# Residual of the second feed-forward on GpSimd, a new order of VectorE's work, and the first turns through DRAM begun earlier

## What is computed

```python
# layer 0: one head
h = film(rmsnorm(x, norm1_w), cond, film1_w, film1_b)
x = x + softmax(Q(h) @ K(h).T / 16) @ V(h) @ proj_w + proj_b
h = film(rmsnorm(x, norm2_w), cond, film2_w, film2_b)
x = x + gelu(h @ mlp_w1 + mlp_b1) @ mlp_w2 + mlp_b2        # hidden 1024, exact gelu
# layer 1: 16 heads of 16 channels
x = x + gate_msa * (attention(modulate(ln(x), shift_msa, scale_msa)) @ w_proj + b_proj)
x = x + gate_mlp * (gelu(modulate(ln(x), shift_mlp, scale_mlp) @ w_mlp1 + b_mlp1) @ w_mlp2 + b_mlp2)
```

## Time and profile before

| what | value |
|---|---|
| median of 3 runs | 1588.21 us (1586.55 to 1589.85) |
| the profiled execution: its time, its span | 1593.56 us, 1591.7 us |
| busy: TensorE, VectorE, ScalarE, GpSimd | 98%, 82%, 53%, 30% |
| chain that ended last, by engine | TensorE 90%, VectorE 6%, ScalarE 2%, issue 1% |
| the same by line, largest | L208 63%, L1728 8%, L1710 7%, L1672 5% |
| mean granted TensorE clock | 0.992 of full speed |

### The profile page before, as it was taken

The page is one execution under the profiler, slowest core; times in us unless marked ns, Lnnn a source line. Parts: engine busy times, 40 slices in busy tenths (PEclk is TensorE's granted clock), DMA queues, the critical chain, the costliest instruction groups (busy, mean ns, idle before and its releaser), DMA issues.

```text
span 1591.7 us, 42636 instructions
## 1 busy us (share of the span) xinstructions
PE 1556.0 (98%) x14322; PEld 1393.5 (88%) x14322; DVE 1299.0 (82%) x2951; ACT 844.9 (53%) x1696; POOL 480.9 (30%) x639
## 2 busy tenths in 40 slices
PE   7999998999999998999999999999998999999999
PEld 7999998999999997777777777777766999999999
DVE  5798888687777777888888888888884888888886
ACT  3666664333333344677767677767765333333333
POOL 2333322131121223234334344333424222222221
PEclk9999999999999999999999999999998999999999
DMA  6600002111111112333333233333331233222222
GB/s 182 211 20 20 21 19 57 68 43 49 44 53 48 44 53 66 106 101 107 105 106 112 96 106 106 102 111 101 102 109 40 81 100 94 92 92 92 92 92 68
DMA packets 145922, 131.67 MB, mean 83 GB/s; under 512 B 23392, under 2 KB 128800, under 8 KB 145840
## 3 DMA queue, kind: packets, MB, share of 16 engines
q1 hardware_dynamic: 145680, 130.56, 25.9%
q0 software_dynamic: 160, 0.04, 0.1%
HBM read 54.09 MB, written 24.02 MB: 49 GB/s over the span
## 4 chain that ended last, share of the span: by engine, by line
PE 90%; DVE 6%; ACT 2%; issue 1%; DVEq 0%; DMA 0%; POOL 0%; ACTq 0%; SPq 0%
PE bank L208 63%; PE bank L1728 8%; PE bank L1710 7%; PE bank L1672 5%; PE bank L1738 2%; PE bank L390 2%; PE bank L1746 1%; PE bank L760 1%; PE bank L463 1%; DVE D_g_hi L1066 1%; PE bank L190 1%; DVE D_g_lo L1068 1%; ACT D_g L1058 0%; DVEq L340 0%; DMA A_w_film<-in_L_cond_film_w 0%
## 5 line engine op out<-in xcount | busy, mean ns | idle before, releaser
L1819 ACT ACTIVATE C_probs<-bank 128x1024 f32<-128x1024 f32 x256 | 262.4, 1025 | 156.3 <-PE bank L1710 156.0
L1684 DVE TENSOR_REDUCE C_negmax<-bank 128x4 f32<-128x1024 f32 x248 | 303.2, 1223 | 47.5 <-PE bank L1672 44.0
L1058 ACT ACTIVATE D_g<-bank,D_bias 128x256 f32<-128x256 f32 x256 | 107.3, 471 | 228.9 <-PE bank L208 210.9
L1058 ACT ACTIVATE B_g<-bank,B_bias 128x256 f32<-128x256 f32 x256 | 107.4, 471 | 222.9 <-PE bank L208 222.9
L357 POOL TENSOR_TENSOR m_small<-m_small,consts 128x2 f32<-128x2 f32 x64 | 48.1, 751 | 463.9 <-DVE m_small L348 236.2
L208 PE MATMUL bank<-D_wt_w_hi,D_g_lo 128*128 128x256 f32 x512 | 145.4, 284 | 4.4 <-DVE D_g_lo L1068 3.8
L208 PE MATMUL bank<-B_wt_w_hi,B_g_lo 128*128 128x256 f32 x512 | 143.7, 281 | 3.9 <-DVE B_g_lo L1068 3.7
L1710 PEld LDWEIGHTS bank<-C_qs,C_kx 64*128 64x128 f32 x1024 | 77.5, 185 | 78.1 <-ACT C_probs L1819 45.6
L208 PE MATMUL bank<-m_h_hi,D_wt_w_lo 128*128 128x256 f32 x512 | 143.3, 280 | 0.8 <-DVE m_h_lo L409 0.8
L208 PE MATMUL bank<-m_h_hi,B_wt_w_lo 128*128 128x256 f32 x512 | 142.7, 279 | 1.2 <-DVE m_h_lo L305 1.2
L208 PE MATMUL bank<-D_wt_w_lo,D_g_hi 128*128 128x256 f32 x512 | 142.8, 279 | 0.0
(11 more groups left out here) (263 smaller groups left out, 4918.5 us busy)
## 6 DMA issues: line engine op xcount, KB each, us to landing
C_qs<-C_q_hi SPq DMA_DIRECT2D x128, 128.0 KB
C_kx<-C_k_hi SPq DMA_DIRECT2D x128, 128.0 KB, 2.5
C_qs<-C_q_lo SPq DMA_DIRECT2D x64, 128.0 KB
C_kx<-C_k_lo SPq DMA_DIRECT2D x64, 128.0 KB, 2.2
C_gbc<-mod_rows SPq DMA_DIRECT2D x32, 256.0 KB, 3.3
D_gbc<-mod_rows SPq DMA_DIRECT2D x32, 256.0 KB, 3.4
out<-xres SPq DMA_DIRECT2D x31, 256.0 KB, 3.5
turned<-N_blocks SPq DMA_DIRECT2D x30, 256.0 KB, 2.0
```

The source lines that it names most:

```text
L1058: ins = eng.activation(o, p, func, bias=per_seq(bias1, 2 * u + d, b))
L1684: e_max.by(eng.tensor_reduce(m4[:, :, :, j], spair[:, :].rearrange("p (e q k) -> p e q k", e=2, q=TH), AX, ALU.max, negate=True))
L1819: e_exp.by(eng.activation(probs[t % NP][:, :], stpair[:, :], ACT.Exp, scale=scl))
```

## The change

- `residual` is new: in D, VectorE makes only `tmp`; xres = tmp + xb is one GpSimd instruction of 128x512, before `add_bias` in GpSimd's list.
- VectorE's order, in both feed-forwards: stats n, split 0, residual (D: `tmp`), split 1, evac_lo f, first half of normalize n, split 2, second half, turn n, split 3. In the first iteration stats of n come after split 1.
- ScalarE's evac_hi goes between gelu 1 and gelu 2.
- The turn begins with sequence START: TensorE's transposes in the feed-forwards go. stats, root, normalize, turn, send and fetch of that sequence are done in the end of the attention before (`B ...1`, `D ...2`). In C the fetch waits for the residual of sequence 30.
- D's `back` and `blocks` are placed elsewhere, behind gaps; A's `b_gate` is allocated later.

```diff
-            def normalize(self, eng, b):
-                self.e_rstd.wait(eng, b)
-                self.e_T.wait(eng, b.back(1))
+            def normalize(self, eng, b, parts=range(TH)):
+                if 0 in parts:
+                    self.e_rstd.wait(eng, b)
+                    self.e_T.wait(eng, b.back(1))
...
-                for h in range(TH):
+                for h in parts:
...
-                NEXT_DVE = {"B stats": 523, "B xhat": 536.5, "B lo": 541, "B stats1": 556, "B split0": 557}
-                NEXT_POOL = {"B root": 527, "B root1": 557}
+                NEXT_DVE = {"B stats": 523, "B xhat": 536.5, "B lo": 541, "B stats1": 540, "B xhat1": 552,
+                            "B turn1": 552.5, "B split0": 557}
+                NEXT_POOL = {"B root": 527, "B root1": 540.5}
+                NEXT_SP = {"B turn1": 553}
...
+                    def b_turn(b):
+                        heads["B"].turn.send(eng, SECOND)
+                        heads["B"].turn.fetch(eng, SECOND)
...
+                if l1:
+                    sb("gap_back", [P, GAP_BACK])
+                    back = sb("back", [P, TH * D])
+                    sb("gap_blocks", [P, GAP_BLOCKS])
+                    blocks = sb("blocks", [P, TH * D])
+                else:
+                    blocks, back = prep.blocks, prep.back
...
-                blocks, back = (sb("blocks", [P, TH * D]), sb("back", [P, TH * D])) if l1 else (prep.blocks, prep.back)
-                turn = Turn(norm, event, START + 1, blocks, back)
+                turn = Turn(norm, event, START, blocks, back)
...
+                def residual(eng, r):
+                    e_xb.wait(eng, r)
+                    e_tmp.wait(eng, r)
+                    x = xres[:, :].rearrange("p (b n) -> p b n", n=TH * D)[:, r.num]
+                    e_res.by(eng.tensor_tensor(x, tmp, xb[r.par][:, :], ALU.add))
...
-                        if f.exists(NB) and not turn.turns(f):
-                            norm.e_lo.wait(eng, f.back(1))
-                            norm.transpose(eng, f)
...
-                        for u in range(1 if last == START else 0, 3):
+                        for u in range(1 if last == START else 0, 2):
                             gelu(eng, m, u)
+                        if f.exists(NB):
+                            turn.evac_hi(eng, f)
+                        gelu(eng, m, 2)
...
-                        if f.exists(NB):
-                            (turn if turn.turns(f) else norm).evac_hi(eng, f)
...
-                        if not turn.turns(f):
-                            if last != START:
-                                norm.stats(eng, f)
-                        elif n.exists(NB):
+                        if n.exists(NB) and last != START:
...
-                                e_tmp.wait(eng, r)
-                                e_res.by(eng.tensor_tensor(x_at(r), t3, x3, ALU.add))
...
                         split(eng, m, 1)
+                        if last == START:
+                            norm.stats(eng, n)
...
-                        if not turn.turns(f):
-                            norm.normalize(eng, f)
-                        elif n.exists(NB):
-                            norm.normalize(eng, n)
+                        if f.exists(NB):
+                            turn.evac_lo(eng, f)
+                        if n.exists(NB):
+                            norm.normalize(eng, n, (0,))
                         split(eng, m, 2)
+                        if n.exists(NB):
+                            norm.normalize(eng, n, (1,))
+                            turn.turn(eng, n)
                         if last == NB:
...
-                        if f.exists(NB):
-                            (turn if turn.turns(f) else norm).evac_lo(eng, f)
-                        if n.exists(NB) and turn.turns(f):
-                            turn.turn(eng, n)
...
-                        if not turn.turns(f):
-                            norm.stats(eng, n)
-                            norm.normalize(eng, n)
-                            turn.turn(eng, n)
...
-                        n, f = i.back(-1), i
-                        if not turn.turns(f):
-                            if last != START:
-                                norm.root(eng, f)
-                        elif n.exists(NB):
+                        n, m, r = i.back(-1), i.back(1), i.back(2)
+                        if n.exists(NB):
                             norm.root(eng, n)
                         if last == 1:
                             prev.e_res.wait(eng, LAST)
-                        m = i.back(1)
+                        if l1 and r.exists(NB) and not final(r):
+                            residual(eng, r)
...
-                        if not turn.turns(f):
-                            norm.root(eng, n)
...
-                            "D lo1": 546, "D split0": 562, "D split1": 563, "D split2": 564, "D split3": 565}
-                NEXT_POOL = {"D root": 517, "D root1": 532, "D w2 lo0": 551, "D w2 lo1": 551.5, "D w2 lo2": 552,
+                            "D lo1": 546, "D stats2": 547, "D xhat2": 549, "D turn2": 549.5, "D split0": 562, "D split1": 563, "D split2": 564, "D split3": 565}
+                NEXT_POOL = {"D root": 517, "D root1": 532, "D root2": 548, "D w2 lo0": 551, "D w2 lo1": 551.5, "D w2 lo2": 552,
                              "D w2 lo3": 557, "D xb": 567}
-                NEXT_SP = {"D w2": 532, "D gates": 555, "D gates1": 556}
+                NEXT_SP = {"D w2": 532, "D turn2": 550, "D gates": 555, "D gates1": 556}
...
+                    def d_turn(b):
+                        heads["D"].turn.send(eng, THIRD)
+                        e_res.wait(eng, Seq(None, NB - 2))
+                        heads["D"].turn.fetch(eng, THIRD)
```

More of the change, by code:

```diff
@@ L32 @@
 Y_GAP = 32
+GAP_BACK, GAP_BLOCKS = 4368, 1024
 class Seq:
@@ L143, in build @@
         heads = {}
-        FIRST, SECOND, LAST = Seq(None, 0), Seq(None, 1), Seq(None, NB - 1)
+        FIRST, SECOND, THIRD, LAST = (Seq(None, n) for n in (0, 1, 2, NB - 1))
         class Weight:
@@ L699, in phase_l0_attention @@
                 xb = [sb(f"xb{u}", [P, TH * D]) for u in range(UNROLL)]
+                b_gate = sb("b_gate", [NB, 2 * D])
                 w_m, w_vp = sb("w_m", [P, KT * D]), sb("w_vp", [P, KT * D])
@@ L859, in vector @@
                         "B lo": lambda b: heads["B"].norm.evac_lo(eng, b),
-                        "B stats1": lambda b: heads["B"].norm.stats(eng, SECOND), "B split0": lambda b: heads["B"].split(eng, b, 0),
+                        "B stats1": lambda b: heads["B"].norm.stats(eng, SECOND),
+                        "B xhat1": lambda b: heads["B"].norm.normalize(eng, SECOND),
+                        "B turn1": lambda b: heads["B"].turn.turn(eng, SECOND), "B split0": lambda b: heads["B"].split(eng, b, 0),
                         "modulation": lambda b: late_modulation(eng), "gate sums": lambda b: gate_sums(eng),
@@ L914, in late_loads @@
                         mlp.load_biases(eng)
+                    def b_turn(b):
+                        heads["B"].turn.send(eng, SECOND)
+                        heads["B"].turn.fetch(eng, SECOND)
                     start_sync(eng)
-                    run_tasks(eng, schedule(EARLY, T_SP, LATE_SP), {
+                    run_tasks(eng, schedule(EARLY, T_SP, LATE_SP, NEXT_SP), {
+                        "B turn1": b_turn,
                         "row": load_row, "film2": load_film2, "ada": load_ada, "late loads": late_loads} | {
                             f"x{c}": lambda b, c=c: load_x(eng, X_FIRST + c * X_CHUNK, X_CHUNK, x_in[3][0])
-                            for c in range(1, X_REST)}, once=LATE_SP)
+                            for c in range(1, X_REST)}, once=LATE_SP | NEXT_SP)
                 phase = Phase(tensor, scalar, vector, gpsimd, sync)
@@ L1278, in phase_mlp @@
                 phase = Phase(tensor, scalar, vector, gpsimd, sync)
-                phase.norm, phase.e_res, phase.head_bank, phase.w2 = norm, e_res, head_bank, w2
+                phase.norm, phase.turn, phase.e_res, phase.head_bank, phase.w2 = norm, turn, e_res, head_bank, w2
                 phase.up, phase.down, phase.gelu, phase.split = up, down, gelu, split
@@ L1941, in d_stats @@
                     def d_stats(b, seq):
-                        e_res.wait(eng, SECOND)
+                        e_res.wait(eng, THIRD)
                         heads["D"].norm.stats(eng, seq)
                     tasks |= {"D stats": lambda b: d_stats(b, FIRST), "D stats1": lambda b: d_stats(b, SECOND),
+                              "D stats2": lambda b: d_stats(b, THIRD), "D xhat2": lambda b: heads["D"].norm.normalize(eng, THIRD),
+                              "D turn2": lambda b: heads["D"].turn.turn(eng, THIRD),
                               "D xhat": lambda b: heads["D"].norm.normalize(eng, FIRST),
@@ L2000, in gpsimd @@
                         "D root": lambda b: heads["D"].norm.root(eng, FIRST),
```

(5 more changed lines are left out.)

6 lines of the change are left out of this document (3 added, 3 removed).

## The result

The changed kernel took 1608.11 us (median of 4, 1606.93 to 1609.14), the kernel before on the same chip 1588.27 (4 runs, 1586.55 to 1589.85): ratio 1.0102, 95% interval 1.0059 to 1.0146. It is slower, as forecast, but by 19.8 us between the medians and not 8.6, and 1608.11 lies 2 us above the range. The medians divide to 1.0125; the ratio as it stands on record, 1.0102, is 16.2 us, and 1604.4 would lie inside the range. The profiled execution took 1608.05 (span 1606.2); that of before stood 5.3 above its median, so the two traces differ by 14.5 us only.

What follows compares the result with a forecast made beforehand. TensorE, 98% busy, bounds the kernel; only the second feed-forward's loop loses pace, waiting for VectorE's split 1 behind GpSimd. 3.4 + 6.2 + 0.6 - 0.8 - 0.8 = +8.6 us on 1588.21 gives 1596.8; eight-in-ten range 1580 to 1606.

Steps and rivals of the forecast that it cites:

- Residual to GpSimd, written-out: Second feed-forward's written-out iterations: GpSimd's bias addition gets between cast and subtraction, +0.43 us each, +3.4 over 8.
- Loop: Second feed-forward's register loop: matmul waits of 0.84 us an iteration against 0.5 today, +0.31 by 20, +6.2 us.
- Rivals 1 and 2: 1: VectorE's cast-subtraction pair stays together, 1582.6 us, chance 0.12; 2: freed 0.69 us removes loop's loss, 1575, chance 0.08.
- Handovers: Starts of both feed-forwards: first turns moved into the attentions' ends remove TensorE stalls but add waits, net -0.8 us each.
- the wait of `lo_y`: Second attention's end: `lo_y` of sequence 30 waits behind GpSimd's root2; TensorE stands 2.6 us, +2.3 after partial payback.
- The stall before 1251.38: Start of the second feed-forward: TensorE's 2.38 us idle on split 0 of a sequence goes.
- The forecast's own lower bound, -5: Second feed-forward's handover: lower bound on its net of -0.8 us; the upper bound was +3.
- the 2.65 us stall: Start of the first feed-forward: TensorE's idle before 266.14 goes, but split 2 waits some 2 us for a landing.
- rivals 3 and 4: 3: both handover stalls fully returned, 1585 to 1588 us, chance 0.15; 4: wait on root2 spreads, 1602, chance 0.15.
- The failed step: First feed-forward, VectorE's new order: subtraction ends about +2.4, split 2 not delayed, GpSimd's work unchanged, cost 0.
- 0.118 "as in part of the loop": Second feed-forward's loop, upper bound +0.65 an iteration: stalls leave following matmuls at 0.118 us instead of 0.113.

Runs made afterwards that it cites:

- e2: The changed kernel with the second feed-forward's residual back on VectorE: 1595.11 us, ratio 1.0019 to the kernel before.
- e9: The kernel before with only the second feed-forward's residual moved to GpSimd, ahead of its bias additions: 1602.04 us, ratio 1.0045.
- e7: The changed kernel with GpSimd's bias additions of the second feed-forward waiting for the low part of split 1, residual still on GpSimd: 1602.69 us, 1.0032.
- e10: The changed kernel with GpSimd's `D root2` moved behind `lo_y` of sequence 30 (slot 550.5 instead of 548): 1604.05 us, ratio 1.0053.
- the second comparison: The changed kernel unchanged, timed again in ten runs beside the kernel before on one chip: 1608.64 us, ratio 1.0072.
- e3: The changed kernel with one added TensorE wait for split 2's low part, just before the first feed-forward's loop: 1602.25 us, ratio 1.0083.
- e6: The kernel before with GpSimd's bias additions of the second feed-forward waiting for the low part of split 1 instead of split 0: 1592.47 us, 0.9978.
- e12: The changed kernel with residual on VectorE, later bias additions, `D root2` behind `lo_y`, and a short TensorE wait before the first feed-forward's loop: 1589.56 us, 0.996.
- The three deliberate stalls: TensorE waits added before the first feed-forward's loop: changed kernel 1602.25 us, kernel before 1591.75 us, changed kernel with three further edits 1589.56 us.

## Why the prediction was right, and where it failed

*Residual to GpSimd, written-out:* +0.43 an iteration forecast, by a bias addition that slips between cast and subtraction; the trace has 11.37 against 10.88, +0.49, the mechanism to the row, and e2 and e9 show that it is this part alone. *Loop:* +6.2 forecast, +5.9 measured (228.2 to 234.2). The difference is right, its two levels were not: the forecast set 0.84 us an iteration of waits against 0.5, and TensorE's intervals have 0.68 against 0.38, with 0.15 of slow pace on top in both kernels. The sentence from the Trainium skill (SBUF — State Buffer, "Who interferes with whom") and the earlier trace rows agree with the rows shown here: a VectorE cast or subtraction stands for as long as a GpSimd addition runs (the cast to 1316.72 behind the residual that ends at 1316.44). Rivals 1 and 2 are out. e7 narrows it: taking the bias additions away from the pair does not free it, the residual is in front of it as well.

*Handovers:* the wait of `lo_y` came where forecast, 2.48 us of TensorE for 2.6, worth about 2 in e10 for +2.3, and a stall of 1.24 us followed at split 2 of the first sequence. The stall before 1251.38 is gone and 1244 to 1262 runs at granted clock 1.00 where 1238 to 1255 had 0.90: D0-3 is 2.3 us shorter in spite of three slower iterations. B31-D0 and D0-3 give -1.3 in the pair of traces, and without the steady loss in D0-3 (3 x 0.49) -2.7, against -0.8. But B31-D0 is 616.8 against 615.8 in the pair and 617.1 against 614.9 in the mean of the seven traces with the wait and the four with the old order, which takes one microsecond of that back. (The forecast's own lower bound, -5, does not come out of its terms, which give -1.5.) In the first feed-forward the 2.65 us stall became one of 1.8 behind the landing; B0-8 and B28-31 give -1.5 and -1.4 (though the arrival of the first one varies from 251.4 to 255.1 over all traces). So the handovers gave something, as forecast; how much more than forecast is not resolved against this scatter, and rivals 3 and 4 did not decide.

*The failed step* is "First feed-forward: the subtraction ends about +2.4, split 2 is not delayed: 0; its GpSimd work is unchanged". It is, but VectorE's work was moved to meet it: evac_lo now runs beside the weight subtraction and ahead of split 2, and takes 1.79. That alone costs a few tenths of a microsecond. The price is the second one, a term that the sum did not have: behind each wait TensorE takes one of two paces and keeps it, and the loop behind has no wait that would change it. 20 sequences times 0.43 make 8.6; the kernel before has 0.9 us of waits near the end of this stage that the changed one does not have, and B8-28 grows by 7.6 (218.6 to 226.1). The forecast knew of both paces (0.118 "as in part of the loop") but only as a bound within the second feed-forward; it took a stretch with no stall for one at full speed. With +7.6 its +8.6 become +16.2; the medians of the first comparison differ by 19.8, the profiled pair by 14.5, and the second comparison gives 1.0072, 11.5 us.

What is shown and what is argued: nine of nine traces with the new order and without e3's long stall have the slow pace from about 360 on, four of four with the old order the fast one, and e3 shows that the order does not force it. That the repeated small waits of the new order give repeated draws, of which the slow result is the one that ends them (at that pace little is late any more), fits all traces but was not tried by itself. What in TensorE makes the two paces stays open.

## What to carry to other kernels

Before an instruction is moved on VectorE, list what GpSimd does beside its new place in each phase, the written-out iterations too; a port conflict moves with it. An engine at 100% busy and full clock can still be 4% slow: count its instructions per microsecond, not its busy share. And a gain from removed stalls is to be measured stage by stage: here e6 removed all of one loop's stalls and kept a quarter of what the loop had lost.

## What the hardware showed that was not expected

TensorE has two steady paces at the granted clock 1.00 (2.4 GHz): one 256-column matmul every 0.1133 or every 0.1178 us, with the same work and neighbours. The pace changes at a wait, one of 0.1 us being enough, and rarely elsewhere (once in e12, near 348.7, at an interval of 0.128). It holds over 20 sequences, 1900 matmuls. In the fourteen traces of the second feed-forward, 303 stalls of 0.25 us or more lie between two clear spells: 224 left the fast pace, 79 the slow one, with nearly the same odds behind a fast spell (147 of 196) as behind a slow one (77 of 107). Of the 175 shorter ones (0.125 to 0.25 us) 105 left the fast pace and 70 the slow one. So in this count a short wait leaves the slow pace more often. The three deliberate stalls left fast (2.7 us), fast (2.4) and slow (1.2). The interval that follows a stall gives a hint: 0.223 or 0.224 went mostly with the fast pace, 0.226 with the slow, 0.221 and 0.222 with either.
